# Layer 0 of a graph network: edge attributes loaded straight into the message columns, without a buffer and a ScalarE copy

## What is computed

```python
edge_index = jnp.stack([src, dst])
h = jnp.maximum(_layernorm(x, axis=-1), 0.0)
x = x + _L0_gnn_ref(h, L0_weight, L0_h_bias, L0_loop_weight, src, dst, edge_type_16)   # relational
h = jnp.maximum(_layernorm(x, axis=-1), 0.0)
x = x + _L1_gnn_ref(h, src, dst, L1_W, L1_b)                                           # plain sum
h = jnp.maximum(_layernorm(x, axis=-1), 0.0)
x = x + _L2_gnn_ref(h, edge_attr_32, src, dst, ...)                                    # MLP on each edge
h = jnp.maximum(_layernorm(x, axis=-1), 0.0)
x = x + _L3_gnn_ref(h, edge_index, edge_attr_32, ...)                                  # [x[src], attr] @ W1
```

## Time and profile before

| | us |
|---|---|
| median of 3 runs | 6812.92 (6805.47 to 6816.28) |
| profiled execution, span from first to last instruction | 5708.1 |
| layer 0, from its first gather to layer 1's first gather | 237.2 to 2301.2 |
| GpSimd busy in the span | 3970.7 (70%) |
| TensorE matmuls busy | 4160.7 (73%) |
| VectorE busy | 2423.5 (42%) |
| ScalarE busy | 2068.2 (36%) |

### The profile page before, as it was taken

The page is one execution under the profiler, slowest core; times in us unless marked ns, Lnnn a source line. Parts: engine busy times, 40 slices in busy tenths (PEclk is TensorE's granted clock), DMA queues, the critical chain, the costliest instruction groups (busy, mean ns, idle before and its releaser), DMA issues. The chain is left out here.

```text
span 5708.1 us, 77858 instructions
## 1 busy us (share of the span) xinstructions
PE 4160.7 (73%) x24814; PEld 2651.7 (46%) x24815; DVE 2423.5 (42%) x6394; ACT 2068.2 (36%) x3761; POOL 3970.7 (70%) x4128
## 2 busy tenths in 40 slices
PE   5776676666677776789966666667677777778985
PEld 3443444333344333345534555555556555544442
DVE  7654444444455553445443223333333333333433
ACT  4543444444467774011113333333333334300000
POOL 0377777777777777677725777777777777767773
PEclk8867767887867887899967999999998999889996
DMA  5643333333344443767722222222232233276762
GB/s 180 244 86 80 84 86 88 91 89 90 92 122 137 137 141 104 264 238 260 251 55 73 79 80 80 82 82 80 83 86 83 82 86 86 83 240 230 262 235 54
DMA packets 571727, 725.68 MB, mean 127 GB/s; under 512 B 180309, under 2 KB 471610, under 8 KB 551884
## 3 DMA queue, kind: packets, MB, share of 16 engines
q1 hardware_dynamic: 372282, 506.05, 26.4%
q0 software_dynamic: 131072, 185.86, 13.4%
q10 hardware_dynamic: 67986, 28.96, 1.9%
HBM read 518.78 MB, written 201.58 MB: 126 GB/s over the span
## 5 line engine op out<-in xcount | busy, mean ns | idle before, releaser
L1130 POOL DMA_INDIRECT layer_msg<-snd_table,idx_src x1536 | 1454.6, 947 | 590.0 <-issue 463.5
L1130 POOL DMA_INDIRECT layer_msg<-rel_table,idx_rel x1536 | 1526.2, 994 | 486.9 <-issue 463.6
L1848 PE MATMUL layer_sum_ps<-layer_sel,layer_msg 128*128 128x128 f32 (+14 forms) x8192 | 993.9, 269 | 1133.9 <-DVE layer_hidden_acc L1544 550.1
L1848 PEld LDWEIGHTS layer_sum_ps<-layer_sel,layer_msg 128*97 128x97 f32 (+2 forms) x8192 | 891.9, 184 | 1388.1 <-issue 1342.9
L1350 ACT CAST layer_frames<-layer_unit_ps 128x700 fp8e4<-128x700 f32 (+9 forms) x1268 | 938.8, 785 | 938.2 <-PE layer_unit_ps L1872 860.9
L1872 PE MATMUL layer_unit_ps<-layer_frame_hot,layer_low_hot 128*128 128x350 bf16 (+9 forms) x3792 | 1010.2, 413 | 133.5 <-ACT layer_frames L1350 121.4
L1130 POOL DMA_INDIRECT layer_msg<-h_table,idx_src x896 | 849.0, 948 | 328.9 <-issue 267.9
L1888 PE MATMUL layer_panel_ps<-layer_piece,layer_pairs 128*128 128x504 fp8e4 (+9 forms) x3920 | 880.1, 381 | 38.1 <-DMA layer_piece<-counts 38.1
L1535 DVE TENSOR_TENSOR layer_msg<-layer_pre_ps,layer_msg 128x512 f32<-128x512 f32 x392 | 271.0, 691 | 1267.7 <-DMA layer_msg<-snd_table,idx_src 1176.0
L1872 PEld LDWEIGHTS layer_unit_ps<-layer_frame_hot,layer_low_hot 128*128 128x128 bf16 x3792 | 400.9, 123 | 591.2 <-ACT layer_frames L1350 287.8
L1888 PEld LDWEIGHTS layer_panel_ps<-layer_piece,layer_pairs 128*128 128x128 f16 x3920 | 376.2, 98 | 476.4 <-issue 67.8
(11 more groups left out here) (238 smaller groups left out, 3544.6 us busy)
## 6 DMA issues: line engine op xcount, KB each, us to landing
layer_piece<-counts SPq DMA_DIRECT2D x48, 1575.0 KB
layer_attr<-in_edge_attr_dram SPq DMA_DIRECT2D x790, 64.0 KB
rel_table<-first_rows SPq DMA_DIRECT2D x98, 512.0 KB, 2.7
layer_piece<-counts SPq DMA_DIRECT2D x24, 1500.0 KB
layer_piece<-counts SPq DMA_DIRECT2D x16, 1593.8 KB
layer_rcv<-rcv_table SPq DMA_DIRECT2D x396, 64.0 KB, 1.8
layer_piece<-counts SPq DMA_DIRECT2D x16, 1543.8 KB
layer_msg<-rel_table,idx_rel POOLq DMA_INDIRECT x1536
```

The source lines that it names most:

```text
L1130: nc.gpsimd.indirect_dma_start(msg[g][:, u, 0:2 * D if dense else width], None, of, bass.IndirectOffsetOnAxis(ap=idx[:, at:at + 1], axis=0 ...
L1848: last = nc.tensor.matmul(sum_ps[g % 2][0:sums, 0:span], msg[g][:, u, c0:c1], sel[j][:, u, 0:span], start=n_part == 0, stop=n_part == len( ...
```

## The change

The buffers `attr` of layer 0 and the ScalarE function `place_attr` are gone. SyncE loads the attributes straight into columns 64 to 95 of `msg[g]`. Since these columns are 128 bytes in each of the four tiles of a partition, a load is now 512 runs of 128 bytes. The load waits for `summed`, as the gather into the same buffer does. TensorE waits for the load itself (`attr_in`), and once, at the start, for the eight columns of ones that ScalarE writes. Layer 2, which has attributes too, uses the same functions with its own buffers and waits, as before.

```diff
-        attr = [sb(f"attr{j}", [P, TILES * FE]) for j in range(SLOTS)] if layer in (0, 2) else None
+        attr = [sb(f"attr{j}", [P, TILES * FE]) for j in range(SLOTS)] if mlp else None
...
+                def attr_at(g, parts=P):
+                    if mlp:
+                        return attr[g % SLOTS][0:parts, :].rearrange("p (u f) -> p u f", u=TILES)
+                    return msg[g][0:parts, :, D:D + FE]
+
+                def attr_free(number):
+                    if mlp:
+                        sp.wait_ge(flipped, number + 1)
+                    else:
+                        sp.wait_ge(summed, number + SLOT_PER)
...
                 def load_attr_group(q):
                     g, group = q % PER, FIRST * PER + q
-                    j = g % SLOTS
-                    sp.wait_ge(flipped if mlp else attr_ready, q + 1)
+                    attr_free(q)
...
-                        sp.dma_start(attr[j][:, :], groups[min(group, full - 1)]).then_inc(attr_in[g], 16)
+                        sp.dma_start(attr_at(g), groups[min(group, full - 1)]).then_inc(attr_in[g], 16)
...
                 if layer == 0:
-                    act.sem_inc(attr_ready, SLOTS)
                     for g in range(PER):
                         nc.scalar.activation(msg[g][:, :, D + FE:D + FE + 1],
-                                             ident[:, 0:TILES].unsqueeze(2), ACT.Copy, bias=1.0, scale=0.0)
+                                             ident[:, 0:TILES].unsqueeze(2), ACT.Copy, bias=1.0, scale=0.0
+                                             ).then_inc(ones_placed, 1)
...
-                def place_attr(n, g):
-                    j = g % SLOTS
-                    act.wait_ge(attr_in[g], n * 16 + 16)
-                    act.wait_ge(summed, n * PER + g + SLOT_PER)
-                    nc.scalar.copy(msg[g][:, :, D:D + FE],
-                                   attr[j][:, :].rearrange("p (u f) -> p u f", u=TILES)).then_inc(attr_ready, 1)
...
                 pe.sem_inc(summed, PER)
+                if layer == 0:
+                    pe.wait_ge(ones_placed, PER)
...
                     if layer == 0:
-                        pe.wait_ge(attr_ready, n * PER + g + 1 + SLOTS)
+                        pe.wait_ge(attr_in[g], n * 16 + 16)
```

More of the change, by code:

```diff
@@ L914, in layer_phase @@
     if layer == 0:
-        attr_ready = sem(name + "attr_ready")
+        ones_placed = sem(name + "ones_placed")
     if mlp:
@@ L1156, in _ @@
                 tail_parts = (E - full * GE) // TILES
-                groups = edge_attr[0:full * GE, :].rearrange("(g p u) f -> g p (u f)", p=P, u=TILES)
+                groups = edge_attr[0:full * GE, :].rearrange("(g p u) f -> g p u f", p=P, u=TILES)
                 def load_idx(i, g):
@@ L1170, in load_attr @@
                                                 skip_runtime_bounds_check_because="i is below ITERS")
-                        sp.dma_start(attr[j][:, :],
-                                     groups[bass.ds(at, 1)].rearrange("a p f -> (a p) f")
+                        sp.dma_start(attr_at(g), groups[bass.ds(at, 1)].rearrange("a p u f -> (a p) u f")
                                      ).then_inc(attr_in[g], 16)
@@ L1181, in load_attr @@
                                 skip_runtime_bounds_check_because="i is below the last iteration")
-                            sp.dma_start(attr[j][:, :],
-                                         groups[bass.ds(safe, 1)].rearrange("a p f -> (a p) f")
+                            sp.dma_start(attr_at(g), groups[bass.ds(safe, 1)].rearrange("a p u f -> (a p) u f")
                                          ).then_inc(attr_in[g], 16)
@@ L1186, in load_attr @@
                             if (ITERS - 1) * PER + g == full:
-                                sp.dma_start(attr[j][0:tail_parts, :],
-                                             edge_attr[full * GE:E, :].rearrange("(p u) f -> p (u f)",
-                                                                                 u=TILES)
+                                sp.dma_start(attr_at(g, tail_parts),
+                                             edge_attr[full * GE:E, :].rearrange("(p u) f -> p u f", u=TILES)
                                              ).then_inc(attr_in[g], 16)
                             else:
-                                sp.dma_start(attr[j][:, :], groups[full - 1]).then_inc(attr_in[g], 16)
+                                sp.dma_start(attr_at(g), groups[full - 1]).then_inc(attr_in[g], 16)
                     if mlp:
                         sp.wait_ge(pre_ready, n * PER + g + 1)
-                        sp.dma_start(rcv[j][:, :],
+                        sp.dma_start(rcv[g % SLOTS][:, :],
                                      table[1][bass.ds(base, P), :]).then_inc(rcv_in[g], 16)
@@ L1274, in _ @@
                             load_idx(i + 1, g)
-                            if attr is None:
+                            if dense:
                                 continue
@@ L1290, in _ @@
                 sp.sem_inc(branch_begun, 1)
-                for loaded in (attr_in[0:SLOTS] if attr else []) + (rcv_in[0:SLOTS] if mlp else []):
+                for loaded in ([] if dense else attr_in[0:SLOTS]) + (rcv_in[0:SLOTS] if mlp else []):
                     sp.wait_ge(loaded, all_attr)
@@ L1352, in edges @@
                 def edges(n, p, i):
-                    if layer == 0:
-                        for g in range(PER):
-                            place_attr(n, g)
                     if mlp:
```

10 lines of the change are left out of this document (3 added, 7 removed).

## The result

| | before | after |
|---|---|---|
| median, us (18 runs each) | 6809.43 (6792.52 to 6824.20) | 6837.89 (6819.32 to 6861.29) |
| ratio, 95% interval | | 1.0043 [1.0033, 1.0053] |
| the profiled execution: span, us | 6800.3 (a new trace) | 6837.4 |
| layer 0, first gather to layer 1's first gather, us | 2398.6 | 2429.7 |
| the rest of the span from there, us | 4163.7 | 4168.3 |

No difference was predicted, 6813 us. The changed kernel takes 28 us more, and its time lies above the range's upper end of 6833.

The account below looks back on a forecast made before the run. GpSimd's issue of gathers was taken to bound layer 0; terms of 0 + 0 + 0 + 0 on a span of 5708.1 us, plus 1104.8 us around it, gave 6813 us, range 6794 to 6833.

Parts of the forecast that it names:

- 1104.8 us lie around the span: Whole run: median 6812.92 us less profiled span 5708.1 us, taken as time outside the span and carried over unchanged.
- so it is never held back: GpSimd in layer 0: waited for TensorE only 4.3 us in 14 waits, so its gather issue sets the pace.
- The copies, 0: ScalarE in layer 0: 392 copies, 119 us of work, hidden by gather issue; gain 0 to 4.3 us, taken as 0.
- The loads into `msg`, 0: SyncE's loads in layer 0, now 512 runs of 128 bytes: issuing, DMA engines and landing each put at 0 us.
- Loads, DMA engines: DMA queues in layer 0: 128-byte packets take 8.6 to 28 ns, low half; share up 1 to 13 points, 0 us.
- Landing and the waits, 0: End of layer 0 and SyncE's and TensorE's moved waits: later landing at most 3.9 us once, taken as 0; waits 0.
- Rival 4: GpSimd's gather issue in layer 0: small packets hold gathers up by 9 ns each, 14 us, 6827; chance 0.04.
- Rivals 1 and 2: Layer 0 gathers beside `frame_hot`: fewer collisions, 6795, chance 0.09; more collisions, 6833, chance 0.08.
- bounds of 985 to 1003: Layer 0's 1536 gathers: mean stays within these ns; leaving them would show the prediction wrong.
- Rival 3: ScalarE is the pace from 1650 us on: 115 groups lose 0.304 us each, 35 us, time 6778; chance 0.03.
- The tail: End of layer 0, from 2271.6 us to layer 1's first gather at 2301.2 us: growth would show the prediction wrong.
- a new wait for TensorE: GpSimd in the changed profile: such a wait, from a late attribute load, would show the prediction wrong.

Follow-up runs that it names:

- e3: Changed kernel without the copy, each load back to 128 runs of 512 bytes into buffers nobody reads, attributes left out of the sums; 1.0002 of before.
- e7: Changed kernel with its 512 runs of 128 bytes going to buffers nobody reads, TensorE not waiting for the loads except the last ones; 1.0036 of before.
- e9: Changed kernel without the copy, each load only 128 runs of 256 bytes, one per partition, into buffers nobody reads; 0.9998 of before.
- e10: Changed kernel without the copy, each load 256 runs of 512 bytes, two per partition with a gap, into buffers nobody reads; 1.0030 of before.
- e14: Changed kernel with each group's load split into four, one per tile, 128 runs of 128 bytes each, into the same places of `msg`; 1.0012 of before.

## Why the prediction was wrong, point by point

**"1104.8 us lie around the span", and "so it is never held back": the first step that failed.** In after 1.8 us lie around the span (6839.21 less 6837.4), and in the new profile of before as well. The 1104.8 us were time inside the span that the profiled execution didn't take. The bound was read from an execution in which TensorE had a clock of 0.76 from 400 to 1600 us, where the new traces have 0.67 and 0.68. There GpSimd waited 4.3 us for TensorE; in the new trace of before it waits 359 us. All the cover that the prediction counted on, GpSimd's issue ahead of a TensorE that has time, was not there. A gap of a sixth between the span and the median was in the text, and it should have been taken as a sign that this trace is of another kind of execution. Whether loads in pieces would cost anything in one like the first isn't known: no later trace is of that kind.

**The copies, 0: right in size, for another reason.** e3 has 1.0002. The reason given was GpSimd's issue as the pace, and it isn't that in an ordinary execution. ScalarE has room there, with 444 us of waits for TensorE in layer 0, and 392 copies of 303 ns fit in.

**The loads into `msg`, 0: the term that was mis-sized.** It should have been +28 us. The prediction weighed the packets' size and number and the time of SyncE, each against rows, and each of these was right to be put at nothing. That an instruction in pieces could cost something that no row of its queue shows stood in no term. The row that bears on it was taken as reassurance: the counts stores, in 128 x 4 runs, issue in 377 ns, less than a plain load. It didn't carry over to loads, which issue in 546 ns when they are in pieces.

**Loads, DMA engines: right.** Packets of 128 bytes take 13 ns by the median (27 ns for one of 512), in the low half of 8.6 to 28 ns. Queue 1 has 151,920 packets more (395 loads of 384 more and the last one's 240; the prediction's 397 loads are 396), and the share in 400 to 1600 us rises from 0.34 to 0.36. The next lines are queue 1 of before and of after:

```profile
q1 hardware_dynamic: 372282, 506.05, 22.3%
```

```profile
q1 hardware_dynamic: 524202, 506.05, 23.1%
```

**Landing and the waits, 0: right.** e7, without TensorE's wait, loses nearly as much (1.0036), and e3, with all waits of the changed kernel, loses nothing.

**Rival 4, small packets.** The Trainium skill ("DMA: Bandwidth & Descriptors", Specifications and "Why small descriptors are slow (HBM only)") holds that transfers below 512 bytes don't reach line rate and that every packet carries a fixed overhead. The rule's sign was right and its mechanism was not the one here: 256 bytes cost nothing (e9, 0.9998), and 512 bytes in two pieces cost 0.30% (e10). Rival 4 gave 6827 for the same reason and with the same fault; it also wanted gathers that take longer, and they take 994 ns.

**Rivals 1 and 2, collisions.** The mean gather was 991 to 998 ns in all kernels, within the bounds of 985 to 1003; collisions neither gained nor lost. In the first trace the 764 gathers beside a `frame_hot` take 1038 ns on average and the 772 others 949; in after 747 take 1045 and 789 take 946. That rival 2's 6833 comes nearest to the measured 6838 is chance. **Rival 3**, ScalarE as the pace, falls with e3: 35 us less would be 0.995.

**The tail** is 43.7 us in the new trace of before and 45.8 in after, not 29.5. All new traces have 38 to 48 us, so the 2 us more are within what it varies by, and the sign of being wrong that was tied to it can't be read. Neither can "a new wait for TensorE": the wait was there before the change.

## What to carry to other kernels

Compare the span of a profiled execution with the median of the runs before reading a bound from it: where they lie a sixth apart, who waits for whom may be the other way round. A copy on an engine with time cost nothing here, and the DMA that replaces it isn't free just because its bytes are the same. Where a DMA has to write several pieces in a partition, try one plain load for each of them against one load of all: here four plain ones took three quarters of the loss away, though they were no faster than the old load with its copy.

## What was not expected of the hardware

- A load in several pieces for each partition costs 0.30 to 0.43% of this kernel, some 50 to 75 ns for each of 384 loads, for 2, 4 or 8 pieces, 128 to 1024 packets, 64 to 512 bytes, on SyncE's queue (on ScalarE's 0.48%, with the time of its issues in it). With one piece for each partition the cost is not measurable from 256 to 896 bytes.
- The issue of such a load takes 541 to 550 ns by the median; that of a plain one 505, or 446 where four follow each other (e14).
- One kernel's execution spanned 5708.1 us at a mean clock of 0.858 and another 6800.3 us at 0.756, with the same work: 4160.7 against 4621.2 us of TensorE busy. By its records TensorE's work accounts for 461 us of the 1092.
